# Self-attention: TensorE's transposes of the exponentials go ahead of the output projection in each step

## The chip, the cores and the metric

The kernel runs on one core of one Trainium2 chip. The metric is the device time in microseconds (us) from launch to the last store. Five engines work side by side and meet through semaphores: PE (TensorE: matmuls and transposes; PEld is its weight load, which overlaps them), DVE (VectorE), ACT (ScalarE), POOL (GpSimd) and SP (SyncE, which issues DMAs).

## What is computed

Four transformer blocks in a row over 64 sequences of 64 tokens with 256 features. The change lies in the causal self-attention of blocks 1 and 3, which is the same code called twice:

```python
x = rms_norm(hidden_states, ln_in_w)
mixed = jnp.where(vm, x @ v_qkv, x @ l_qkv)          # two experts, chosen by token
q, k, v = heads(q), heads(k), heads(v)               # 16 heads of 16
q, k = apply_rotary(q, k, position_ids, l)
ctx = sdpa(q, k, v, causal=True)                     # softmax(q k^T / 4) v
attn_out = jnp.where(vm, ctx @ v_dense, ctx @ l_dense)
hidden_states = residual + attn_out
```

## The kernel before

The 64 sequences are worked as 32 pairs of 64 + 64 tokens, so one pair fills 128 partitions. The nine phases of the network run one after the other (`layer0`, `self_attention(1)`, cross attention, gated feed-forward, latent attention, GELU feed-forward, `self_attention(3)`, cross attention, gated feed-forward). All engines wait for the last residual of a phase (`previous_done`) before they begin the next.

Inside `self_attention` every engine has its own hand-written list, and the order of the calls in it is the order on the engine. There is no scheduler. The lists are software pipelines: in step p of its loop (p = 0 to 33), PE has, before the change,

- `scores(p)` (L1021, L1029): two bf16 matmuls that write the causal mask into `ps_s`, and 16 matmuls on 64x64 tiles for q k^T;
- `dense(p - 2)` (L1075 to L1077): the output projection, six 128x512 matmuls into bank `ps_b`;
- `probs_t(p - 1)` (L1043): eight transposes of the exponentials into banks `ps_p` and `ps_d`;
- `proj_qk(p + 2)` (L984 to L986): twelve 128x512 matmuls into `ps_a`;
- `pv(p - 1)` (L1059): 64 small matmuls, exponentials times v;
- `xt_(p + 3)` (L972), `proj_v(p + 2)` (L1000 to L1002), `out_t(p - 1)` (L1066) and `qk_t(p + 2)` (L1013).

Calls whose pair lies outside 0 to 31 are left out. So steps 0 and 1 have no `dense`, steps 30 and 31 have no projections, step 32 has only `dense(30)`, `probs_t(31)`, `pv(31)` and `out_t(31)`, and step 33 only `dense(31)`.

The waits that matter here:

- `probs_t(p - 1)` waits for the exponentials (`exp_ok`, ACT L524) and for `on_ok` (DVE L1288). Its second four transposes also wait for `qkt_ok` up to pair p + 2, the copy of `ps_d` by ACT (L1154, `qkt_copy`) after `qk_t(p + 2)`, the last thing PE did in the step before.
- ACT copies the transposed exponentials out of both banks (L1162, `pt_copy`), and then makes the exponentials of pair p (L524). `pv(p - 1)` waits for both copies.
- `dense(p - 2)` waits for `o_ok`: `out_t` on PE, then `out_high` on ACT (L1169), then `out_low` on DVE (L1294). From pair 29 on it also waits for the residual before it.
- DVE takes `dense`'s result in `residual(p - 2)` (L1300, L1303), between `softmax_front(p)` (L510, L516) and `rope_products(p + 2)` (L1271). `proj_v(p + 2)` writes `ps_b` again and waits for that residual.

Of the kernel before, what the change touches and what calls it, by code (L numbers as in the profile page):

```python
# [107 lines left out]
def build(nc, t):  # L108
    with ExitStack() as ctx:
# [173 lines left out]
        def has(p):  # L283

            return not isinstance(p, int) or 0 <= p < PAIRS
# [626 lines left out]
        def self_attention(n, loaded, load_next):  # L912
            with ExitStack() as own:
# [50 lines left out]
                def _(pe):  # L964
                    previous_done(pe)
                    def xt_(p):
                        pe.wait_ge(xn_ok.handle, xn_ok.at(p + 1))
                        if xlow_ok.due(p):
                            pe.wait_ge(xlow_ok.handle, xlow_ok.at(p))
                        for c in range(CH):  # L970
                            for e in range(2):
                                ins = nc.tensor.transpose(ps_t[:, (2 * c + e) * P:(2 * c + e + 1) * P],  # L972
                                                          xn[:, e, c * P:c * P + P], ident)
                        ins.then_inc(xt_pe.handle, 1)

                    def proj_qk(p):

                        pe.wait_ge(xlow_ok.handle, xlow_ok.at(p + 1))
                        if rope1.due(p):
                            pe.wait_ge(rope1.handle, rope1.at(p))  # L980
                        u = p % 2
                        for k in range(2 * CH):
                            e, c = divmod(k, CH)
                            nc.tensor.matmul(ps_a[:], xh[:, u, c, e], wh[:, k, 0:2 * D], start=(k == 0), stop=False)  # L984
                            nc.tensor.matmul(ps_a[:], xh[:, u, c, e], wl[:, k, 0:2 * D], start=False, stop=False)  # L985
                            ins = nc.tensor.matmul(ps_a[:], xl[:, u, c, e], wh[:, k, 0:2 * D], start=False,  # L986
                                                   stop=(k == 2 * CH - 1))
                        ins.then_inc(qk_pe.handle, 1)

                    def proj_v(p):  # L990

                        if v_ok.due(p):
                            pe.wait_ge(v_ok.handle, v_ok.at(p))
                        if res_ok.due(p - 3):
                            pe.wait_ge(res_ok.handle, res_ok.at(p - 3))
                        u = p % 2
                        for k in range(2 * CH):
                            e, c = divmod(k, CH)
                            out = ps_b[:, 0:D]
                            nc.tensor.matmul(out, xh[:, u, c, e], wh[:, k, 2 * D:3 * D], start=(k == 0), stop=False)  # L1000
                            nc.tensor.matmul(out, xh[:, u, c, e], wl[:, k, 2 * D:3 * D], start=False, stop=False)
                            ins = nc.tensor.matmul(out, xl[:, u, c, e], wh[:, k, 2 * D:3 * D], start=False,  # L1002
                                                   stop=(k == 2 * CH - 1))
                        ins.then_inc(v_pe.handle, 1)
# [11 lines left out]
                    def scores(p):  # L1016
                        pe.wait_ge(kx_ok.handle, kx_ok.at(p + 1))
                        if sub_ok.due(p):
                            pe.wait_ge(sub_ok.handle, sub_ok.at(p))
                        for r in range(2):  # L1020
                            nc.tensor.matmul(ps_s[:, 512 * r:512 * r + 512], ident_b[:],  # L1021
                                             causal_b[:].unsqueeze(1).broadcast_to([P, 8, S]),
                                             start=True, stop=False, skip_group_check=True)
                        for r in range(2):
                            rows = slice(S * r, S * r + S)
                            for c in range(CH):
                                for b in range(2):
                                    at = 512 * r + 256 * c
                                    ins = nc.tensor.matmul(ps_s[b * S:b * S + S, at:at + 4 * S],  # L1029
                                                           qkt[rows, p % 2, c, b * S:b * S + S],  # L1030
                                                           kx[rows, p % 2, c, b].rearrange("p h k -> p (h k)"),
                                                           start=False, stop=True, skip_group_check=True)
                            ins.then_inc(s_pe.handle, 1)

                    def probs_t(p):
                        for r, bank in enumerate((ps_p, ps_d)):
                            pe.wait_ge(exp_ok.handle, exp_ok.at(p, r + 1))
                            if r == 0 and on_ok.due(p):
                                pe.wait_ge(on_ok.handle, on_ok.at(p))
                            if r == 1:  # L1040
                                pe.wait_ge(qkt_ok.handle, qkt_ok.at(min(p + 3, PAIRS)))
                            for j in range(4):
                                ins = nc.tensor.transpose(bank[:, j * P:j * P + P],  # L1043
                                                          probs[:, p % 2, (4 * r + j) * P:(4 * r + j + 1) * P], ident)
                            ins.then_inc(pt_pe.handle, 1)

                    def pv(p):

                        pe.wait_ge(pt_ok.handle, pt_ok.at(p + 1))
                        wait_slot(pe, p)  # L1050
                        if o_ok.due(p):
                            pe.wait_ge(o_ok.handle, o_ok.at(p))
                        for j in range(J):
                            at = 4 * (j % 4 // 2) + 2 * (j // 4) + j % 2
                            for h in range(2):
                                rows = slice(S * h, S * h + S)
                                for b in range(2):
                                    v = (v_own if b == h else v_swap)[rows, p % VS, 2 * j + h]
                                    ins = nc.tensor.matmul(o_at[b * S:b * S + S, h, j], pt[rows, at, b * S:b * S + S], v,  # L1059
                                                           start=True, stop=True, skip_group_check=True)  # L1060
                        ins.then_inc(pv_pe.handle, 2)
# [7 lines left out]
                    def dense(p):  # L1069
                        pe.wait_ge(o_ok.handle, o_ok.at(p + 1))  # L1070
                        pe.wait_ge(v_ok.handle, v_ok.at(min(p + 4, PAIRS)))
                        if p >= PAIRS - 3:
                            pe.wait_ge(res_ok.handle, res_ok.at(p))
                        for c in range(CH):
                            nc.tensor.matmul(ps_b[:], oth[:, c], oh[:, c], start=(c == 0), stop=False)  # L1075
                            nc.tensor.matmul(ps_b[:], oth[:, c], ol[:, c], start=False, stop=False)
                            ins = nc.tensor.matmul(ps_b[:], otl[:, c], oh[:, c], start=False, stop=(c == CH - 1))  # L1077
                        ins.then_inc(d_pe.handle, 1)
# [12 lines left out]
                    for p in range(PAIRS + 2):  # L1091
                        if has(p):
                            scores(p)
                        if has(p - 2):
                            dense(p - 2)
                        if has(p - 1):
                            probs_t(p - 1)
                        if has(p + 2):
                            proj_qk(p + 2)
                        if has(p - 1):  # L1100
                            pv(p - 1)
                        if has(p + 3):
                            xt_(p + 3)
                        if has(p + 2):
                            proj_v(p + 2)
                        if has(p - 1):
                            out_t(p - 1)
                        if has(p + 2):
                            qk_t(p + 2)
# [1550 lines left out]
```

## Time and profile before

| | us |
|---|---|
| Time, median of 3 runs (lowest, highest) | 2440.89 (2437.07, 2441.07) |
| Time of the profiled execution | 2433.26 |
| Its span, first to last instruction | 2431.5 |
| PE busy | 2269.9 (93%) |
| DVE busy | 1401.2 (58%) |
| ACT busy | 1142.3 (47%) |
| POOL busy | 653.4 (27%) |

The profile shows one execution. Busy time says how long an engine had work in hand. It does not say that the engine's work set the end: for that one reads the stage in question in order of time, and asks at each start whether the instruction waited for another engine or only for its turn. The mean TensorE clock granted over the span was 0.966 of full speed. The first self-attention phase lies at about 171 to 523 us of the span, the second at about 1651 to 2004 us.

### The profile page before, as it was taken

How to read it: one execution, taken by the hardware profiler on the slowest of the kernel's cores; microseconds unless marked ns; L12 is line 12 of the kernel's file. 1: busy time of each engine (PE TensorE's matmuls, PEld its weight loads, DVE VectorE, ACT ScalarE, POOL GpSimd, SP SyncE). 2: the span in 40 equal slices, each digit the busy share in tenths (PEclk: the TensorE clock that was granted, in tenths of full speed). 3: DMA queues.
4: the chain of work that ended last, by engine and by line, in shares of the span. 5: the costliest groups of instructions: out<-in, count | busy, mean ns of one | idle time of the engine just before them, and what ended most of it. 6: DMA issues, size and time to landing. Idle time of an engine off the chain costs nothing.

```text
span 2431.5 us, 62427 instructions
## 1 busy us (share of the span) xinstructions
PE 2269.9 (93%) x24066; PEld 1841.4 (76%) x24067; DVE 1401.2 (58%) x2837; ACT 1142.3 (47%) x2617; POOL 653.4 (27%) x833
## 2 busy tenths in 40 slices
PE   5969999979979997999999979998999989998998
PEld 3647888857659996788888859996888866667998
DVE  4756666647763333666666555545666655764333
ACT  3765445437653332444344335445455436664333
POOL 1552222226642221111111110002222215652222
PEclk9989999979989998999999989998999998999999
DMA  6620000020022113000000010000000002001111
GB/s 199 81 37 18 16 16 15 14 76 24 28 82 61 58 58 129 5 2 2 2 2 2 2 36 1 0 0 19 16 16 13 16 13 83 26 30 59 58 58 42
DMA packets 78750, 85.79 MB, mean 35 GB/s; under 512 B 19907, under 2 KB 69648, under 8 KB 78384
## 3 DMA queue, kind: packets, MB, share of 16 engines
q1 hardware_dynamic: 56016, 41.55, 7.3%
q10 hardware_dynamic: 14128, 19.74, 2.6%
q0 software_dynamic: 8368, 21.15, 2.4%
q8 instruction: 172, 2.82, 0.5%
q14 instruction: 66, 0.54, 0.1%
HBM read 52.35 MB, written 21.40 MB: 30 GB/s over the span
## 4 chain that ended last, share of the span: by engine, by line
PE 85%; DVE 4%; ACT 2%; issue 1%; ACTq 1%; POOL 0%; DMA 0%; POOLq 0%; DVEq 0%; SPq 0%
PE ps_all L2200 3%; PE ps_all L2202 3%; PE ps_all L2201 3%; PE ps_all L1431 3%; PE ps_all L1059 3%; PE ps_all L1457 3%; PE ps_all L1029 3%; PE ps_all L1832 3%; PE ps_all L1443 3%; PE ps_all L984 3%; PE ps_all L985 2%; PE ps_all L986 2%; PE ps_all L1043 2%; PE ps_all L2225 2%; PE ps_all L2227 2%; PE ps_all L2226 2%
## 5 line engine op out<-in xcount | busy, mean ns | idle before, releaser
L1224 POOL TENSOR_TENSOR s_kx<-s_qkt,const 128x512 f32<-128x512 f32 x128 | 131.6, 1049 | 448.0 <-ACT s_qkt L1154 448.0
L539 POOL TENSOR_TENSOR a_probs<-a_probs,a_sm 128x1024 f32<-128x1024 f32 x32 | 60.9, 1904 | 385.0 <-DVE a_sm L534 385.0
L1580 POOL TENSOR_TENSOR c_kx<-c_qkt,const 128x512 f32<-128x512 f32 x128 | 130.6, 1037 | 118.1 <-ACT c_qkt L1523 117.9
L2200 PE MATMUL ps_all<-f_wh,f_xh 128*128 x396 | 154.4, 390 | 5.3 <-DVE f_xl L2348 5.3
L1162 ACT ACTIVATE s_pt<-ps_all 128x512 f32<-128x512 f32 x128 | 69.6, 595 | 185.8 <-PE ps_all L1043 185.8
L2201 PE MATMUL ps_all<-f_wh,f_xl 128*128 x396 | 148.5, 375 | 0.0
L2202 PE MATMUL ps_all<-f_wl,f_xh 128*128 x396 | 148.5, 375 | 0.0
L1921 ACT ACTIVATE self_w<-ps_all,a_q_bias 128x256 f32<-128x256 f32 x128 | 53.8, 471 | 196.7 <-PE ps_all L1768 196.7
L2343 DVE SCALAR_TENSOR_TENSOR f_h<-ps_all,rstd,f_act_g 128x688 f32<-128x688 f32 x66 | 61.7, 935 | 142.0 <-PE ps_all L2202 128.9
L2225 PE MATMUL ps_all<-f_dh,f_hh 128*128 x396 | 116.9, 295 | 4.0 <-DVE f_hl L2358 4.0
L510 DVE TENSOR_REDUCE s_mx<-ps_all 128x8 f32<-128x512 f32 x128 | 82.5, 686 | 60.6 <-PE ps_all L1029 60.6
L2264 ACT ACTIVATE f_act_g<-ps_all,rstd 128x688 f32<-128x688 f32 x66 | 55.2, 837 | 131.8 <-PE ps_all L2202 131.7
L2269 ACT ACTIVATE f_hh<-ps_all 128x768 fp32r<-128x768 f32 x66 | 53.7, 813 | 132.4 <-PE ps_all L2210 132.4
L1271 DVE TENSOR_TENSOR s_roped<-ps_all,rope 128x512 f32<-128x512 f32 x64 | 44.3, 692 | 120.2 <-PE ps_all L986 120.2
L984 PE MATMUL ps_all<-s_wh,s_xh 128*128 128x512 f32 x256 | 107.2, 419 | 6.5 <-DVE s_xl L1256 6.5
L2227 PE MATMUL ps_all<-f_dl,f_hh 128*128 x396 | 111.6, 282 | 0.0
L2226 PE MATMUL ps_all<-f_dh,f_hl 128*128 x396 | 111.3, 281 | 0.0
L1531 ACT ACTIVATE c_pt<-ps_all 128x512 f32<-128x512 f32 x128 | 69.5, 594 | 82.6 <-PE ps_all L1443 82.6
L1630 DVE TENSOR_REDUCE c_mx<-ps_all 128x8 f32<-128x512 f32 x128 | 82.5, 686 | 44.7 <-PE ps_all L1431 44.5
L1136 ACT ACTIVATE s_xh<-ps_all 128x512 fp32r<-128x512 f32 x64 | 38.4, 600 | 143.8 <-PE ps_all L972 143.8
L985 PE MATMUL ps_all<-s_wl,s_xh 128*128 128x512 f32 x256 | 101.6, 397 | 0.0
L986 PE MATMUL ps_all<-s_wh,s_xl 128*128 128x512 f32 x256 | 101.5, 396 | 0.0
(319 smaller groups left out, 7423.6 us busy)
## 6 DMA issues: line engine op xcount, KB each, us to landing
s_v_swap<-s_v_own SPq DMA_DIRECT2D x128, 68.0 KB, 2.1
f_x_in<-x_sorted SPq DMA_DIRECT2D x66, 128.0 KB, 2.0
x_res<-x_sorted SPq DMA_DIRECT2D x66, 128.0 KB, 2.1
x_sorted<-x_res POOLq DMA_DIRECT2D x1, 4224.0 KB, 17.2
l_rows<-in_x SPq DMA_DIRECT2D x32, 128.0 KB
x_res<-in_x SPq DMA_DIRECT2D x32, 128.0 KB
x_res<-x_back SPq DMA_DIRECT2D x1, 3584.0 KB, 14.4
l_rows<-in_ctx SPq DMA_DIRECT2D x32, 64.0 KB
```

The costliest lines, as they stand in the source:

```text
L510: nc.vector.tensor_reduce(mx[:, u, half(r)], s3[:, half(r)], op=ALU.max, axis=AX.X) \
L984: nc.tensor.matmul(ps_a[:], xh[:, u, c, e], wh[:, k, 0:2 * D], start=(k == 0), stop=False)
L985: nc.tensor.matmul(ps_a[:], xh[:, u, c, e], wl[:, k, 0:2 * D], start=False, stop=False)
L986: ins = nc.tensor.matmul(ps_a[:], xl[:, u, c, e], wh[:, k, 0:2 * D], start=False, stop=(k == 2 * CH - 1))
L1224: ins = nc.gpsimd.tensor_tensor(kx[:, p % 2, c], qkt[:, p % 2, 2 + c].rearrange("p (b k) -> p b k", b=2).unsqueeze(2) .broadcast_to([P, 2, ...
L1580: ins = nc.gpsimd.tensor_tensor(kx[:, p % 2, b], qkt[:, p % 2, 1, b * S:b * S + S].unsqueeze(1).broadcast_to([P, RH, S]), const[:, C_H8X:C ...
L2200: nc.tensor.matmul(bank, x_high, wh[:, w_at], start=(c == 0), stop=False)
L2201: nc.tensor.matmul(bank, x_low, wh[:, w_at], start=False, stop=False)
L2202: ins = nc.tensor.matmul(bank, x_high, wl[:, w_at], start=False, stop=(c == CH - 1))
L2225: nc.tensor.matmul(bank, high, dh[:, w_at], start=(m == 0), stop=False)
L2226: nc.tensor.matmul(bank, low, dh[:, w_at], start=False, stop=False)
L2227: ins = nc.tensor.matmul(bank, high, dl[:, w_at], start=False, stop=(m == IC - 1))
```

## The change

In PE's list `probs_t(p - 1)` and `dense(p - 2)` change places. Nothing else does: the other engines' lists, the semaphores and the number of instructions are the same.

```diff
                     for p in range(PAIRS + 2):
                         if has(p):
                             scores(p)
+                        if has(p - 1):
+                            probs_t(p - 1)
                         if has(p - 2):
                             dense(p - 2)
-                        if has(p - 1):
-                            probs_t(p - 1)
                         if has(p + 2):
                             proj_qk(p + 2)
```

PE's rows in step 2 of the first self-attention, the first step that has both calls (- before, + after; the projection of pair 4, L984, follows):

```order
 L1021 MATMUL ps_all<-causal_b,ident_b 128x512
 L1029 MATMUL ps_all<-s_kx,s_qkt 64x256 x8
+L1043 MATMUL ps_all<-const,s_probs 128x128 [waits on_ok,exp_ok]
+L1043 MATMUL ps_all<-const,s_probs 128x128 x3
+L1043 MATMUL ps_all<-const,s_probs 128x128 [waits qkt_ok,exp_ok]
+L1043 MATMUL ps_all<-const,s_probs 128x128 x3
 L1075 MATMUL ps_all<-s_oh,s_oth 128x512 [waits v_ok,o_ok]
 L1076 MATMUL ps_all<-s_ol,s_oth 128x512
```

The eight transposes (L1043) stand between the scores and the six matmuls of the projection (L1075 to L1077), and the projection of q and k comes directly behind those. Steps 3 to 31 are alike in this.

PE's rows in step 32 of the first self-attention, where no scores and no projection of q and k are left:

```order
 L1066 MATMUL ps_all<-const,s_on 128x128 [waits on_ok]
 L1066 MATMUL ps_all<-const,s_on 128x128
+L1043 MATMUL ps_all<-const,s_probs 128x128 [waits on_ok,exp_ok]
+L1043 MATMUL ps_all<-const,s_probs 128x128 x3
+L1043 MATMUL ps_all<-const,s_probs 128x128 [waits qkt_ok,exp_ok]
+L1043 MATMUL ps_all<-const,s_probs 128x128 x3
 L1075 MATMUL ps_all<-s_oh,s_oth 128x512 [waits res_ok,v_ok,o_ok]
 L1076 MATMUL ps_all<-s_ol,s_oth 128x512
```

The transposes of pair 31 now stand directly behind `out_t(30)` (L1066) and ahead of `dense(30)`, whose first matmul waits for `o_ok`, which hangs on that same `out_t(30)`.

## Rows read from the trace of the kernel before

**Rows 1.** The page, part 4: shares of the span in the chain that ended last

```profile
PE 85%; DVE 4%; ACT 2%; issue 1%; ACTq 1%; POOL 0%; DMA 0%; POOLq 0%; DVEq 0%; SPq 0%
```

**Rows 2.** Windows, middle of self-attention: length; PE, PEld, DVE, ACT, POOL busy; PEclk; DMA

```profile
240.00:400.00 160.00, 160.00 (x2031) 128.93 (x2029) 106.14 (x216) 80.02 (x186) 36.49 (x42) 1.00 0.06 15
```

**Rows 3.** Timeline, PE, one middle step and the next one's start: start, length, what

```profile
309.03 0.59 PE L1021 MATMUL ps_all<-causal_b,ident_b 128*128 128x512 bf16 x2
...
310.59 0.50 PE L1075 MATMUL ps_all<-s_oh,s_oth 128*128 128x512 f32 x1
310.93 0.39 PE L1076 MATMUL ps_all<-s_ol,s_oth 128*128 128x512 f32 x1
...
312.09 1.03 PE L1043 MATMUL ps_all<-const,s_probs 128*128 128x128 f32 x8
312.88 0.48 PE L984 MATMUL ps_all<-s_wh,s_xh 128*128 128x512 f32 x1
...
313.43 0.39 PE L986 MATMUL ps_all<-s_wh,s_xl 128*128 128x512 f32 x1
...
315.48 0.39 PE L986 MATMUL ps_all<-s_wh,s_xl 128*128 128x512 f32 x1
315.80 0.23 PE L1059 MATMUL ps_all<-s_v_own,s_pt 64*64 64x17 f32 x1
...
319.42 0.59 PE L1021 MATMUL ps_all<-causal_b,ident_b 128*128 128x512 bf16 x2
```

**Rows 4.** Timeline, PE, step 1, which has no output projection

```profile
196.15 0.59 PE L1021 MATMUL ps_all<-causal_b,ident_b 128*128 128x512 bf16 x2
...
197.71 1.09 PE L1043 MATMUL ps_all<-const,s_probs 128*128 128x128 f32 x8
198.56 0.48 PE L984 MATMUL ps_all<-s_wh,s_xh 128*128 128x512 f32 x1
...
199.11 0.39 PE L986 MATMUL ps_all<-s_wh,s_xl 128*128 128x512 f32 x1
```

**Rows 5.** Waits, whole span: waiting group <- releaser: us in total, times, longest

```profile
PEld ps_all L1075 <- issue: 22.4, 58, 0.4
```

**Rows 6.** Timeline, ACT and DVE in the step of rows 3

```profile
309.23 0.60 ACT L1154 ACTIVATE s_qkt<-ps_all 128x512 f32<-128x512 f32 x1
313.70 1.15 ACT L524 ACTIVATE s_probs<-s_probs 128x512 f32<-128x512 f32 x2
...
313.08 0.47 DVE L1300 SCALAR_TENSOR_TENSOR s_part<-ps_all,vm,x_res 128x256 f32<-128x256 f32 x1
...
315.90 0.69 DVE L1271 TENSOR_TENSOR s_roped<-ps_all,rope 128x512 f32<-128x512 f32 x1 [1.82 <-PE ps_all L986]
```

**Rows 7.** Timeline, PE, steps 30 and 32 of the first self-attention

```profile
495.72 0.59 PE L1021 MATMUL ps_all<-causal_b,ident_b 128*128 128x512 bf16 x2
...
498.79 1.03 PE L1043 MATMUL ps_all<-const,s_probs 128*128 128x128 f32 x8
500.56 0.23 PE L1059 MATMUL ps_all<-s_v_own,s_pt 64*64 64x17 f32 x1 [0.74 <-ACT s_pt L1162]
...
509.60 0.44 PE L1066 MATMUL ps_all<-const,s_on 128*128 128x128 f32 x2 [0.84 <-DVE s_on L1288]
...
511.04 0.79 PE L1075 MATMUL ps_all<-s_oh,s_oth 128*128 128x512 f32 x1 [1.00 <-DVE s_otl L1294]
...
513.76 1.23 PE L1043 MATMUL ps_all<-const,s_probs 128*128 128x128 f32 x8
515.73 0.23 PE L1059 MATMUL ps_all<-s_v_own,s_pt 64*64 64x17 f32 x1 [0.74 <-ACT s_pt L1162]
```

**Rows 8.** Windows at the end of the first self-attention, columns as in rows 2

```profile
507.30:510.70 3.40, 1.56 (x66) 1.23 (x66) 1.34 (x5) 1.70 (x4) 0.00 (x0) 1.00 0.02 5
510.70:514.10 3.40, 3.06 (x8) 2.38 (x9) 0.38 (x2) 0.00 (x0) 0.00 (x0) 0.51 0.00 0
514.10:517.50 3.40, 2.01 (x72) 1.68 (x70) 1.41 (x4) 1.09 (x2) 0.00 (x0) 0.99 0.00 0
```

## The prediction

> **What bounds the kernel now.** I first read the shares of the chain that ended last: PE holds 85% of the span, DVE 4%, ACT 2% [rows 1]. Then I ask which engine sets the pace in the stage that the change touches. In 160 us from the middle of the first self-attention PE is busy 160.00 of 160.00 us at full granted clock, while DVE has 106.14, ACT 80.02 and POOL 36.49 [rows 2]. So in a middle step no other engine is waited for, and a reordering can only gain there what TensorE itself loses between one kind of work and the next. Third, I read one middle step in order of time. It takes 319.42 - 309.03 = 10.39 us [rows 3]. Fourth, I look at steps 30 to 33, where the projections have run out: there PE does wait, 0.74 us for ACT's copies before `pv` (L1059), 0.84 us for DVE before `out_t` (L1066), 1.00 us for DVE before `dense` [rows 7]. The reader is to see two different regimes: 28 steps in each phase (2 to 29) paced by PE's own work, and a few last steps paced by a chain through PE, ACT and DVE.
>
> **Part 1: the middle steps.** Nothing is added or removed, so only the seams between groups count. Before, the start of the third matmul of `proj_qk` lies at 313.43 - 309.03 = 4.40 us in the step [rows 3]. Now the same point after the change:
> - Transposes directly behind the scores: step 1 shows this, since it has no `dense`. They start at 197.71 - 196.15 = 1.56 us, and the next group follows 198.56 - 197.71 = 0.85 us later [rows 4], against 312.88 - 312.09 = 0.79 in a middle step [rows 3].
> - So `dense` starts at 1.56 + 0.85 = 2.41. The same kind of matmul directly behind transposes needs 0.55 us from its first to its third start (312.88 to 313.43, and 198.56 to 199.11) [rows 3, 4].
> - All further 128x512 matmuls, those of `dense` and then of `proj_qk`, follow in a steady rhythm: (315.48 - 313.43) / 9 = 0.228 us [rows 3]. From the third of `dense` to the third of `proj_qk` there are six intervals, 1.37 us.
>
> The sum is 2.41 + 0.55 + 1.37 = 4.33, so 0.07 us less than 4.40. The reason can be read from the rows: the first `dense` matmul behind the scores takes 310.93 - 310.59 = 0.34 instead of 0.23 us, and PEld stood idle 0.4 us before it, 58 times [rows 3, 5]. A large matmul there pays for its weight load in the open. A transpose pays only 0.06 (0.85 against 0.79), and the large matmuls then form one unbroken run of 18. 56 steps (28 in each phase) times 0.07 = 4 us. Bounds: nothing, if the seam costs the same whatever follows the scores. At the other end 0.11 us, the whole surcharge, makes 6 us. I take 4, since both orders of neighbours stand in the rows.
>
> The Trainium skill ("TensorE: Matmul & The Clock Gate", section "Step-by-step: what each phase is for") says that TensorE pulls a weight load ahead of matmuls in flight, so the next weights load while the current tile computes. By that rule the order of the groups would not matter and this term would be 0. The row of the weight load's idle time before L1075 differs from it at this seam, so the sum keeps 4.
>
> What covers the waits: the second four transposes wait for ACT's copy of `ps_d`, which ends at 309.23 + 0.60 - 309.03 = 0.80 us in the step [rows 6]. They would now start at about 1.56 + 0.85/2 = 1.99 us, so 1.2 us of cover are left of the 2.7 before. The exponentials were ready much earlier (L524 of the step before ended about 10.39 - (314.85 - 309.03) = 4.6 us ahead of the step's start) [rows 6]. `dense` ends later: its last matmul starts at 2.41 + 0.55 + 3 x 0.228 = 3.64 us. DVE's residual starts at 313.08 - 309.03 = 4.05 now, and would start near 4.1. Behind it DVE has 1.82 us of idle time before L1271, which waits for PE [rows 6]. That delay costs nothing. If the cover on DVE were gone, `proj_qk` of the next step would be late by the same 0.1 us. ACT's copies and the exponentials move about 1.5 us earlier, which nobody on the bounding engine waits for in these steps.
>
> **Part 2: steps 30 and 31.** Without `proj_qk`, `pv` follows the transposes by ACT's two copies: 500.56 - 498.79 = 1.77 us [rows 7]. Before, `dense` (1.50 us, 310.59 to 312.09 [rows 3]) stood in front of that chain, and `pv` started at 500.56 - 495.72 = 4.84 us in the step. After, `dense` lies beside the copies. The chain by the copies: 1.56 + 0.06 + 1.77 = 3.39. The chain by PE: `dense` starts at 2.41, and from the first large matmul behind transposes to `pv` it is (315.80 - 312.88) - 6 x 0.228 = 1.55 us for six of them [rows 3], so 3.96. The later one decides: 4.84 - 3.96 = 0.88 us less. Four such steps give 3.5 us. DVE must fit the residual in before `out_norm`. By the starts above, that fits with about 0.1 us to spare. If not, this term loses 0.4 us in all.
>
> **Part 3: step 32.** Before: `out_t(30)` at 509.60, then 1.44 us until `dense(30)` (through ACT and DVE), 2.72 us until the transposes, 1.97 until `pv(31)` at 515.73, in all 6.13 us [rows 7]. After, the eight transposes and ACT's copies run inside the 1.44 us and beside `dense`: the copies' chain is about 0.25 + 0.06 + 1.77 = 2.1 us. The path is then 1.44 + `dense` + nothing. With `dense` at full clock it is 1.44 + 1.57 = 3.01, a gain of 3.1. At half clock, as in the rows (PEclk 0.51 from 510.7 to 514.1 [rows 8]), it is 1.44 + 2.72 + 0.2 = 4.36, a gain of 1.8. I can't tell which of the two levels (2.4 or 1.2 GHz) holds there, so I take the middle, 2.4, and 4.8 us for both phases. Steps 0, 1 and 33 are unchanged. The second self-attention has the same list, so the same terms. The next phase waits for the last residual, so what is gained reaches the end.
>
> **The sum.** 4 + 3.5 + 4.8 = 12.3 us. The profiled execution took 2433.26 us (span 2431.5), so it would take 2421.0. It lies 7.6 us below the median of the three runs, 2440.89. Against the median the forecast is 2440.89 - 12.3 = 2428.6 us, rounded 2428.5. (0.2%, or 4.9 us, is about what a measurement of this kernel can tell from no change.)
>
> **The rivals.**
> - **The seam is worth nothing** (chance 0.20). The 58 weight-load gaps of 0.4 us [rows 5] may simply move with the scores, and the first transpose then pays what the first `dense` paid. Only parts 2 and 3 remain, 8.3 us: 2432.6. Against it: rows 4. The page on TensorE named above speaks for this one.
> - **The clock takes it back** (0.12). The granted clock went to half after a stretch in which PE was busy 1.56 of 3.40 us [rows 8]. The transposes moved into the gaps of steps 30 to 32 might not count for it, and steps 31 to 33 could see two more such stretches at half in each phase. One stretch of 3.4 us full of PE work costs 1.7 us, four cost 6.8: 12.3 - 6.8 = 5.5, so 2435.4, and a little more of it ends within 0.2%. The Trainium skill (same page, "Part 4: PE-mode transpose") says that transposes don't count as PE being busy. No row here separates them from other work.
> - **The transposes meet a wait of their own: slower** (0.04). The second four wait for ACT's copy of `ps_d`. That copy would have to end at 2.0 us in the step instead of 0.80, for example because another long ACT operation slipped ahead of it. Every microsecond beyond the cover is a microsecond of PE in each of 56 steps. It decides from 1.2 + 0.07 + (3.5 + 4.8 + 4.9)/56 (0.24, what parts 2 and 3 give and the bound of 0.2%) = 1.5 us of delay. At 1.6 us the steps lose 0.33 each, 18 us, less the 8.3 from the ends: 2451. Against it: ACT does this copy right when PE delivers, its list is unchanged, and it is busy half the time [rows 2].
> - **My forecast**: 0.64.
>
> **How the numbers follow.** Faster by over 0.2%: my forecast and the rival without the seam, nearly whole (0.60 + 0.19), and half of the clock's (0.06), 0.85. Within 0.2%: 0.11. Slower: 0.04. The range: the low end is the profiled execution's own level less the largest sum from the bounds (6 + 3.5 + 6.2 = 15.7, 2433.3 - 15.7 = 2418). The high end takes in the clock rival, 2435.4, and a little of the spread of the runs shown (2437.07 to 2441.07): 2437.
>
> **What the profile after would show.** A middle step of 10.32 us instead of 10.39, transposes at 1.56 us, `dense` at 2.41, and six intervals of 0.23 between the third matmul of `dense` and the third of `proj_qk`. PEld's 0.4 us of idle time stands before L1043. ACT's L1162 comes some 1.5 us earlier, DVE's L1300 at about 4.1. In steps 30 and 31 the wait of L1059 for ACT is gone, in step 32 `pv` comes 3.0 to 4.4 us behind `out_t`. Wrong would be: a wait of L1043 for ACT L1154, a middle step that is not shorter, or half-clock stretches that begin before step 32.

## The result and the profile after

| | before | after |
|---|---|---|
| Time, median of 4 runs (lowest, highest), us | 2440.98 (2437.07, 2448.52) | 2422.36 (2419.70, 2426.89) |
| Ratio after / before, 95% interval | | 0.9922 (0.9893 to 0.9951) |
| Profiled execution, us | 2433.26 | 2426.89 |
| Span, mean granted clock | 2431.5, 0.966 | 2425.1, 0.970 |

The kernel got faster by 18.6 us between the medians, 0.78%. The forecast was 12.3 us, or 2428.5 as a median, the range 2418 to 2437. Two later sets of the changed kernel gave 0.9924 (0.9908 to 0.9941) and 0.9934 (0.9921 to 0.9948).

The first lines of the page of after have the form of the table ahead of the prediction and of [rows 1]:

```profile
PE 2264.3 (93%) x24066; PEld 1839.5 (76%) x24067; DVE 1402.9 (58%) x2837; ACT 1153.0 (48%) x2617; POOL 655.0 (27%) x833
...
PE 85%; DVE 4%; ACT 2%; issue 1%; ACTq 1%; POOL 0%; DMA 0%; POOLq 0%; DVEq 0%; SPq 0%
```

These shares hardly moved and tell nothing of where 6.4 us of span went, so the stage itself has to be read. Timeline of after, PE, the same middle step as in [rows 3], to the start of the next:

```profile
308.17 0.59 PE L1021 MATMUL ps_all<-causal_b,ident_b 128*128 128x512 bf16 x2
...
309.73 1.09 PE L1043 MATMUL ps_all<-const,s_probs 128*128 128x128 f32 x8
310.58 0.48 PE L1075 MATMUL ps_all<-s_oh,s_oth 128*128 128x512 f32 x1
310.89 0.39 PE L1076 MATMUL ps_all<-s_ol,s_oth 128*128 128x512 f32 x1
...
312.52 0.40 PE L986 MATMUL ps_all<-s_wh,s_xl 128*128 128x512 f32 x1
...
313.67 0.39 PE L985 MATMUL ps_all<-s_wl,s_xh 128*128 128x512 f32 x1
...
314.58 0.39 PE L986 MATMUL ps_all<-s_wh,s_xl 128*128 128x512 f32 x1
314.89 0.23 PE L1059 MATMUL ps_all<-s_v_own,s_pt 64*64 64x17 f32 x1
...
318.52 0.59 PE L1021 MATMUL ps_all<-causal_b,ident_b 128*128 128x512 bf16 x2
```

The step takes 10.35 us instead of 10.39. The transposes start at 1.56, `dense` at 2.41, the third matmul of `proj_qk` at 4.35, as worked out to within 0.02 us (1.56, 2.41, 4.33). But from the second matmul of `dense` to the eighth of `proj_qk` (310.89 to 313.67) the twelve intervals average 0.232 us, and only the last four (313.67 to 314.58) are 0.228.

Before the change `dense` already had this slower rhythm. Its last matmul in the step of [rows 3] (timeline of before, PE):

```profile
311.86 0.40 PE L1077 MATMUL ps_all<-s_oh,s_otl 128*128 128x512 f32 x1
```

From its second matmul (310.93 [rows 3]) to this sixth one there are four intervals in 0.93 us, 0.233 us each, where `proj_qk` had 0.228.

The wait of the weight load moved with the seam, as its row in the list of waits shows ([rows 5] had L1075, 22.4 us, 58 times):

```profile
PEld ps_all L1043 <- issue: 23.9, 62, 0.4
```

ACT and DVE in that step, timeline of after, against [rows 6]:

```profile
308.37 0.60 ACT L1154 ACTIVATE s_qkt<-ps_all 128x512 f32<-128x512 f32 x1
310.42 1.08 ACT L1162 ACTIVATE s_pt<-ps_all 128x512 f32<-128x512 f32 x2 [1.46 <-PE ps_all L1043]
...
312.25 0.48 DVE L1300 SCALAR_TENSOR_TENSOR s_part<-ps_all,vm,x_res 128x256 f32<-128x256 f32 x1
...
315.00 0.69 DVE L1271 TENSOR_TENSOR s_roped<-ps_all,rope 128x512 f32<-128x512 f32 x1 [1.74 <-PE ps_all L986]
```

ACT's copy L1154 ends 0.80 us into the step, before the transposes start at 1.56, so nothing waits. ACT's L1162 starts at 2.25, 1.45 us earlier than before. DVE's residual starts at 4.08 (forecast 4.1, before 4.05), and DVE still idles 1.74 us behind it.

The last steps of the first self-attention, timeline of after, PE ([rows 7] are those of before):

```profile
504.50 0.59 PE L1021 MATMUL ps_all<-causal_b,ident_b 128*128 128x512 bf16 x2
...
506.06 1.09 PE L1043 MATMUL ps_all<-const,s_probs 128*128 128x128 f32 x8
506.90 0.48 PE L1075 MATMUL ps_all<-s_oh,s_oth 128*128 128x512 f32 x1
...
508.47 0.23 PE L1059 MATMUL ps_all<-s_v_own,s_pt 64*64 64x17 f32 x1
...
516.64 0.44 PE L1066 MATMUL ps_all<-const,s_on 128*128 128x128 f32 x2 [0.84 <-DVE s_on L1288]
516.92 1.04 PE L1043 MATMUL ps_all<-const,s_probs 128*128 128x128 f32 x8
518.09 0.50 PE L1075 MATMUL ps_all<-s_oh,s_oth 128*128 128x512 f32 x1
...
519.68 0.23 PE L1059 MATMUL ps_all<-s_v_own,s_pt 64*64 64x17 f32 x1
...
521.64 0.44 PE L1066 MATMUL ps_all<-const,s_on 128*128 128x128 f32 x2 [0.84 <-DVE s_on L1288]
523.08 0.50 PE L1075 MATMUL ps_all<-s_oh,s_oth 128*128 128x512 f32 x1 [1.00 <-DVE s_otl L1294]
```

Step 30: `pv` starts 3.97 us into the step instead of 4.84, and its wait for ACT is gone. Step 32: from `out_t(30)` at 516.64 to `pv(31)` it is 3.04 us instead of 6.13. The waits for DVE ahead of L1066 and the last L1075 stay, since nothing was put into them. Windows of after, columns as in [rows 2]:

```profile
517.40:520.80 3.40, 3.27 (x76) 2.39 (x73) 1.39 (x3) 1.19 (x3) 0.00 (x0) 1.00 0.02 5
520.80:524.20 3.40, 1.56 (x8) 1.14 (x8) 1.11 (x3) 0.38 (x1) 0.00 (x0) 1.00 0.00 0
528.20:541.80 13.60, 7.58 (x32) 5.03 (x32) 1.92 (x4) 3.72 (x13) 5.26 (x6) 0.50 1.05 304
...
1995.90:2016.40 20.50, 12.33 (x54) 6.78 (x53) 4.82 (x12) 6.11 (x19) 7.41 (x9) 0.50 0.62 206
```

Both `dense(30)` (from 518.09) and `dense(31)` (from 523.08) of this phase ran at the full level, where before the clock was at half from 510.7 to 514.1 us [rows 8] and again from 517.6 us. It falls only at 528.2, when the phase is over (it ends at 525.8). In the second self-attention, which ends at 1997.5 us, it fell at 1995.9, in the last matmul of `dense(31)`.

Cut at PE's own starts, the two self-attention phases of both profiles come apart like this (worked out from the traces, us):

```
                                             before           after
first L972 to scores(2)                   33.91  34.44     34.45  34.23
scores(2) to scores(30), 28 steps        290.63 290.63    289.51 289.51
scores(30) to out_t(30)                   13.87  13.88     12.15  12.15
out_t(30) to pv(31)                        6.13   6.25      3.03   3.03
pv(31) to dense(31)                        3.65   3.40      3.40   3.40
dense(31) to the next phase                4.02   4.03      2.76   2.95
phase                                    352.22 352.63    345.30 345.26
```

### The profile page after: what moved, and what is told of

Its sections match the earlier page's. It is cut to its first block, busy times and chain, and to the rows that moved or that the text cites. A ratio compares the mean times of both kernels' runs of the same rounds, so it can differ in the third digit from the quotient of the medians.

```text
span 2425.1 us, 62427 instructions
## 1 busy us (share of the span) xinstructions
PE 2264.3 (93%) x24066; PEld 1839.5 (76%) x24067; DVE 1402.9 (58%) x2837; ACT 1153.0 (48%) x2617; POOL 655.0 (27%) x833
## 4 chain that ended last, share of the span: by engine, by line
PE 85%; DVE 4%; ACT 2%; issue 1%; ACTq 1%; POOL 0%; DMA 0%; POOLq 0%; DVEq 0%; SPq 0%
PE ps_all L2202 3%; PE ps_all L2201 3%; PE ps_all L2200 3%; PE ps_all L1059 3%; PE ps_all L1457 3%; PE ps_all L1431 3%; PE ps_all L1029 3%; PE ps_all L1043 3%; PE ps_all L1832 3%; PE ps_all L1443 3%; PE ps_all L984 3%; PE ps_all L985 2%; PE ps_all L986 2%; PE ps_all L2225 2%; PE ps_all L2227 2%; PE ps_all L2226 2%
## 5 line engine op out<-in xcount | busy, mean ns | idle before, releaser
L1162 ACT ACTIVATE s_pt<-ps_all 128x512 f32<-128x512 f32 x128 | 69.5, 596 | 90.9 <-PE ps_all L1043 90.8
L984 PE MATMUL ps_all<-s_wh,s_xh 128*128 128x512 f32 x256 | 102.7, 401 | 6.5 <-DVE s_xl L1256 6.5
```

## The experiments

The lengths of stretches, which the experiments are read by, are worked out from the traces. A phase of self-attention runs from its first PE instruction (L972) to the first PE instruction of the next phase. The stretch ahead of it (column "ahead") runs from the first L633 on PE, the start of `layer0`, to the first self-attention.

```
kernel           ratio to before (95%)       ahead   phase 1   phase 3 (us)
before                                       144.5   352.22    352.63
before_again     0.9997 (0.9987 to 1.0006)   152.2   352.38    352.74
mid_only         0.9992 (0.9982 to 1.0001)   146.6   350.84    353.35
steps3031_only   0.9966 (0.9952 to 0.9980)   146.1   349.45    349.49
step32_only      0.9959 (0.9944 to 0.9973)   148.5   347.71    348.20
tail_only        0.9949 (0.9932 to 0.9965)   151.9   346.80    347.04
after            0.9922 (0.9893 to 0.9951)   153.3   345.30    345.26
after_again      0.9924 (0.9908 to 0.9941)   148.0   345.24    345.33
after_third      0.9934 (0.9921 to 0.9948)   148.6   345.23    345.35
early_scores31   0.9940 (0.9922 to 0.9957)   146.2   347.14    345.13
qk_first         0.9932 (0.9918 to 0.9945)   146.3   345.51    345.48
front_sbuf       (one run, 2419.93 us)       147.2   345.22    345.32
```

("Phase 3" is the second self-attention, that of block 3.)

**before_again**, the kernel before without an edit.

> The kernel before, unchanged, once more. All theories: ratio 1 within its interval. What it is for: how far the time up to the first self-attention (171 us in the profile of before, 181 in that of after, with nothing changed there) moves by itself. If that is chance, this run's first self-attention starts somewhere between 165 and 185 us, its length is 352 to 353 us as before, and steps 30 to 32 look as before.

Measured: ratio 0.9997. The first self-attention starts at 178.6 us, where the first profile had 171.2. Where each began and where the last `dense` was, for this kernel and below for the changed one (first and last start of a line's instructions; L1077 within the first 700 us):

```profile
L972 PE MATMUL ps_all<-const,s_xn x256: 270/273/448, 178.6 to 1972.1; 128*128 128x128 f32 x128
...
L1077 PE MATMUL ps_all<-s_oh,s_otl x64: 393/398/628, 214.8 to 529.3; 128*128 128x512 f32 x64
```

```profile
L972 PE MATMUL ps_all<-const,s_xn x256: 270/273/448, 180.5 to 1963.8; 128*128 128x128 f32 x128
...
L1077 PE MATMUL ps_all<-s_oh,s_otl x64: 390/395/399, 217.9 to 524.3; 128*128 128x512 f32 x64
```

From the first to the last L1077 it is 314.5 us before and 306.4 after. The stretch ahead of self-attention varies by 9 us from one execution to another, in kernels that don't differ there (144.5 to 153.3 in the table), while a phase repeats to 0.2 us as long as the clock does. Part of the 9 us is DMA: L633 waits for `x_res` 14.7 us in all in the first profile of before and 19.8 us in that of after. So the 6.4 us between the two spans understate the change: after's profile had the longest such stretch of all, before's the shortest. The two phases together are (352.22 + 352.63) - (345.30 + 345.26) = 14.3 us shorter.

**tail_only**, the new order in steps 30 to 32 alone. In it and the three that follow, a condition on p chooses the order:

```diff
+                        if has(p - 1) and (p >= 30):
+                            probs_t(p - 1)
                         if has(p - 2):
                             dense(p - 2)
-                        if has(p - 1):
+                        if has(p - 1) and not (p >= 30):
                             probs_t(p - 1)
```

> The new order only in steps 30 to 32, the old one in steps 2 to 29. If the gain comes mostly from the last steps (my theory, with the profile after: 0.86 us for each of steps 30 and 31, 3.1 us for step 32, 1.5 us for dense(31) at full clock), each self-attention phase gets 6.3 us shorter and the kernel 12.6 us, ratio 0.995. If the gain were one of the middle steps, this run is within 0.1% of before. Half clock at the end of the phases should be gone as in the profile after.

Measured: ratio 0.9949 (12.4 us), phases 5.4 and 5.6 us shorter, 11 of the 14.3. In the first phase the clock fell just ahead of `dense(31)`, against the expectation. Windows of this kernel:

```profile
517.60:521.00 3.40, 2.18 (x69) 1.43 (x68) 1.65 (x4) 0.35 (x1) 0.00 (x0) 1.00 0.02 5
521.00:524.40 3.40, 2.78 (x6) 1.82 (x6) 0.42 (x1) 0.04 (x1) 0.00 (x0) 0.50 0.00 0
```

`dense(31)`, whose first matmul starts at 521.62, then runs at half: from its start to the next phase it is 4.02 us instead of the 2.76 in after. In the second phase the clock fell within `dense(31)`, and it is 3.35. This is mostly why the phases miss the expected 6.3 us by 0.9 and 0.7.

**mid_only**, `p < 30` in the condition.

> The new order only in steps 2 to 29, the old one in steps 30 to 32. If the middle steps give 0.04 us each (what the profile after shows), the phases get 1.1 us shorter each, 2.2 us in all, ratio 0.999. If they gave what the whole change measured beyond the last steps (18.6 less 12.6), it would be 6 us, ratio 0.9975. Steps 30 to 32 as before, with their waits.

Measured: ratio 0.9992 (1.9 us, but the interval includes no change at all). The profile is sharper than the times: the middle step is 10.353 us instead of 10.393 in steps 2 to 28 of both phases, and step 29, which has no `xt_`, 9.967 instead of 10.007. The first phase is 1.4 us shorter. The second came out 0.6 to 0.7 longer, since one more stretch at half fell into its step 31, as these windows of the kernel show:

```profile
1984.00:1987.90 3.90, 3.90 (x24) 1.84 (x24) 1.16 (x3) 0.38 (x1) 0.00 (x0) 0.62 0.02 4
1987.90:1991.30 3.40, 2.66 (x76) 2.24 (x74) 2.63 (x5) 2.10 (x4) 0.00 (x0) 1.00 0.00 0
```

So the middle steps are worth 0.040 us each, 2.2 us in all, and not the 6 us of the other theory.

**steps3031_only**, `p in (30, 31)`.

> The new order only in steps 30 and 31 of both phases. By part 2 of the prediction, 0.88 us for each of the four, 3.5 us in all, phase length 350.6 us. Together with step 32 alone (phase lengths 347.7 and 348.2) and the middle alone (350.8 and 353.4) this shows whether the parts add up to 345.3. The half-clock stretches of step 32 and of the end stay as before.

Measured: 0.9966, phases 349.45 and 349.49, 2.8 and 3.1 us shorter where 1.8 was expected. From `scores(30)` to `out_t(30)` it is 12.15 us, as in after. The rest came from the clock, which had not been expected to move. Windows of this kernel:

```profile
510.00:513.00 3.00, 2.00 (x12) 1.56 (x11) 0.59 (x2) 0.38 (x1) 0.00 (x0) 1.00 0.03 5
...
516.30:523.00 6.70, 4.31 (x10) 2.42 (x10) 2.08 (x8) 0.38 (x1) 0.10 (x1) 0.50 0.00 0
```

`dense(30)`, in its old place in this kernel (511.13), ran at full clock in both phases. That the steps before it had become denser is the likely reason, since nothing else differs from before.

**step32_only**, `p == 32`.

> The new order only in step 32 of both self-attention phases. If the wait chain behind out_t(30) takes pv(31) with it and the granted clock stays full, 3.1 us come from step 32 and 1.5 us from dense(31) at full clock: 4.6 us a phase, 9.2 us in all, ratio 0.996, phase length 347.7 us. If the clock does not follow (half level as before), 1.8 us a phase, 3.6 us in all, phase length 350.5 us.

Measured: 0.9959, phases 347.71 and 348.20. The first of the two expectations, to 0.5 us. Timeline of this kernel, PE:

```profile
513.35 0.44 PE L1066 MATMUL ps_all<-const,s_on 128*128 128x128 f32 x2 [0.84 <-DVE s_on L1290]
513.63 1.04 PE L1043 MATMUL ps_all<-const,s_probs 128*128 128x128 f32 x8
514.79 0.50 PE L1075 MATMUL ps_all<-s_oh,s_oth 128*128 128x512 f32 x1
...
516.38 0.23 PE L1059 MATMUL ps_all<-s_v_own,s_pt 64*64 64x17 f32 x1
...
519.78 0.50 PE L1075 MATMUL ps_all<-s_oh,s_oth 128*128 128x512 f32 x1 [1.00 <-DVE s_otl L1296]
```

The same 3.03 us from `out_t(30)` to `pv(31)`, and `dense(31)` at full clock. One window of this kernel:

```profile
511.20:514.60 3.40, 2.37 (x74) 2.10 (x74) 1.36 (x4) 1.89 (x5) 0.00 (x0) 1.00 0.03 5
```

Up to `out_t(30)` this kernel ran as before. There the clock fell 1.14 us behind the start of `out_t(30)` (510.74), after 3.40 us in which PE had been busy for 1.56 [rows 8]. Here PE was busy for 2.37 of the 3.40 us up to the same place. What was added are the transposes (from 513.63), and the clock did not fall. This was so in both phases, while in all six phases measured with the old steps 30 to 32 the clock fell 1.1 to 2.4 us behind `out_t(30)`. That speaks for transposes counting as work for the clock. It is no proof, since the moment of the fall moves from one execution to the next. One moved call in one step (times two phases) brings some 9 us, 60% of the whole. The parts overlap: steps 30 and 31 alone (2.9 a phase) and step 32 alone (4.5) would add up to 7.4, together they give 5.5. Each alone already brings `dense(30)` to full clock, which is worth 1.4 us and can be won only once, and in tail_only `dense(31)` was at half again, wholly in one phase and in part in the other.

**after_again** and **after_third**, the changed kernel.

> The changed kernel once more, beside the other three. If the parts add up: 14.5 us faster than before, ratio 0.994 (12.6 from the last steps, 2.2 from the middle ones). If the 18.6 us between the two medians were all the change's, ratio 0.9922 again and a phase length below 345 us.

> The changed kernel a third time, as the partner of early_scores31 and to narrow the ratio. By the lengths of the phases in the profiles, 14.4 us faster than before, ratio 0.994. By the two medians so far, 16 to 19 us, 0.992 to 0.993. Phase length 345.3 us both times.

Measured: 0.9924 and 0.9934, phases 345.2 to 345.4 in both. By the phases the change is worth 14.4 us, 0.59% (ratio 0.9941). That lies inside the intervals of the first and third set and at the very edge of the second. Three medians say 16 to 19 us; the 18.6 of the first set rests on four runs of before with a median of 2440.98, where the later sets of 11 to 19 runs had 2436.6 to 2438.0. What lies behind the start of the first self-attention, without the two phases, took 1555.4 us in both profiles of before and 1554.0, 1555.4 and 1555.3 in the three of after, so no further gain stands there. The rest of the difference would have to lie ahead of self-attention, where executions differ by 9 us, or be chance. Which of the two is not shown.

**early_scores31**, the changed kernel with the scores of pair 31 ahead of `out_t(29)`.

```diff
+                        if p == PAIRS - 2:
+                            scores(p + 1)
                         if has(p - 1):
                             out_t(p - 1)
```

(and `scores(p)` at the head of the step is left out for p = 31).

> The changed kernel, and in step 30 the scores of pair 31 go ahead of out_t(29), into the 0.84 us in which PE waits for DVE there. If that wait is a real hole in the path, step 31 starts about 0.8 us earlier in each phase: 1.6 us, ratio to before 0.9935 where the changed kernel has 0.994. If DVE (front of pair 31 behind out_norm(29)) sets the pace instead, nothing.

Measured: 0.9940 (0.9922 to 0.9957), no better than after. `pv(30)` follows `pv(29)` by 5.66 us instead of 6.22, so the hole was filled. But `out_t(30)` follows `pv(30)` by 2.33 us instead of 1.96, so 0.18 is left of it. `out_t(29)` now stands behind the scores (502.67), DVE's `out_low(29)` waits for it, and the front of pair 31 is queued behind that on DVE, although its scores were ready. Timeline of this kernel, DVE:

```profile
503.63 0.42 DVE L1296 TENSOR_TENSOR s_otl<-ps_all,s_oth 128x256 fp32r<-128x256 f32 x1 [1.68 <-ACT s_oth L1171]
503.97 1.28 DVE L510 TENSOR_REDUCE s_mx<-ps_all 128x8 f32<-128x512 f32 x2
```

The second phase gained some 0.2 us, and the first lost 1.9 to a stretch at half clock. Windows of this kernel, and its timeline, PE:

```profile
507.30:510.70 3.40, 2.67 (x13) 2.37 (x14) 1.06 (x4) 1.58 (x3) 0.00 (x0) 0.72 0.02 5
508.80:512.20 3.40, 3.40 (x11) 2.37 (x9) 0.42 (x1) 1.28 (x3) 0.00 (x0) 0.50 0.02 5
```

```profile
508.03 0.44 PE L1066 MATMUL ps_all<-const,s_on 128*128 128x128 f32 x2 [1.21 <-DVE s_on L1290]
...
512.29 0.23 PE L1059 MATMUL ps_all<-s_v_own,s_pt 64*64 64x17 f32 x1
```

Here `dense(30)` ran at half in the new order, and from `out_t(30)` to `pv(31)` it is 4.26 us instead of 3.03.

**front_sbuf**, the changed kernel with DVE reading other numbers from SBUF in self-attention.

```diff
-                            softmax_front(dve, mx, probs, p, p % 2)
+                            softmax_front(dve, mx, probs, p, p % 2, self_w[:, 0:NH * S])
```

> The changed kernel with one thing altered in self-attention: DVE's maxima and subtractions (L510, L516) read 1024 columns of the raw weights in SBUF in place of the scores in PSUM, so its attention is that of other numbers. It asks why twelve of the large matmuls in a middle step follow at 0.230 to 0.236 us instead of 0.227, which is why the middle step gained 0.04 and not 0.07 us. If DVE's reads of PSUM slow TensorE's writes, the intervals of dense and of the first six of proj_qk fall to 0.227 and a middle step takes 10.31 us. If not, they stay, and the step stays at 10.35.

Measured: the middle step stays at 10.353 us, interval by interval. Timeline of this kernel, PE:

```profile
303.95 0.39 PE L1076 MATMUL ps_all<-s_ol,s_oth 128*128 128x512 f32 x1
...
306.73 0.39 PE L985 MATMUL ps_all<-s_wl,s_xh 128*128 128x512 f32 x1
...
307.64 0.39 PE L986 MATMUL ps_all<-s_wh,s_xl 128*128 128x512 f32 x1
```

Again 2.78 us for twelve intervals and 0.91 for four. DVE's reads of the scores in PSUM are not the reason. The other reads of PSUM, ACT's and those of DVE's residual, were left as they were here.

**qk_first**, the changed kernel with `proj_qk` ahead of `dense`, and on DVE `rope_products` ahead of `residual`.

```diff
-                        if has(p - 2):
-                            dense(p - 2)
                         if has(p + 2):
                             proj_qk(p + 2)
+                        if has(p - 2):
+                            dense(p - 2)
```

> The changed kernel with proj_qk ahead of dense (PE: scores, transposes, proj_qk, dense), and DVE's rope_products ahead of its residual to fit. It asks what the intervals of 0.229 to 0.236 us hang on. If on the place (the first twelve after the transposes are slow whatever they are), the middle step stays at 10.355 us. If on the kind (proj_qk directly behind transposes has two slow intervals in step 1, dense has five everywhere), five fewer are slow and the middle step takes 10.33 us, 1.4 us in all over 56 steps. If residual and proj_v, which waits for it, become the bound, it is slower: half a microsecond a step would be 28 us, ratio above 1.

Measured: 0.9932, the middle step 10.353 us. Timeline of this kernel, PE:

```profile
302.62 0.48 PE L984 MATMUL ps_all<-s_wh,s_xh 128*128 128x512 f32 x1
...
303.40 0.39 PE L984 MATMUL ps_all<-s_wh,s_xh 128*128 128x512 f32 x1
...
305.44 0.40 PE L1075 MATMUL ps_all<-s_oh,s_oth 128*128 128x512 f32 x1
...
306.61 0.39 PE L1077 MATMUL ps_all<-s_oh,s_otl 128*128 128x512 f32 x1
```

Now `proj_qk`, directly behind the transposes, runs at 0.227 us an interval from its fourth on (303.40 to 305.44, nine intervals), and `dense` at 0.234 (305.44 to 306.61, five). So the slow intervals go with `dense` and what follows it, not with the place behind the transposes. The 18 large matmuls take 3.99 us from first to last start instead of 4.00. The 0.01 us is lost again between `proj_v` and `out_t`, so the step as a whole is the same and the expected 10.33 us did not come. Its phases are 0.2 us longer, in step 29 (10.13 us instead of 9.97). None of these versions beats the changed kernel.

## Why the prediction was right

**The two regimes** held: middle steps paced by PE alone, last steps by a chain through PE, ACT and DVE, and the larger part of the gain from the last ones. The mechanism is the one that was forecast. That the sum of 12.3 us lies near the 14.3 of the phases is in part luck, since two errors of opposite sign stand in it. The median, 2422.4 against 2428.5, lies 6 us off: 2 of them are in the phases, the other 4 are the part of the medians' difference that the phases don't hold.

**Part 1, the middle steps (forecast 4 us, measured 2.2).** The seams behave as worked out, to 0.02 us at every point up to the third matmul of `proj_qk`. The step that failed is "All further 128x512 matmuls, those of `dense` and then of `proj_qk`, follow in a steady rhythm", with 0.228 us for it. That rhythm was taken from nine late intervals of `proj_qk`. `dense` has its own of 0.233, which the trace of before already showed (310.93 to 311.86), and behind `dense` the first matmuls of `proj_qk` run at 0.229 to 0.235 too, where behind transposes only two did. That costs 0.03 us a step, about half of it up to the third matmul of `proj_qk` and half behind it. The rival "the seam is worth nothing" is refuted by 0.040 us in each of 56 steps, which mid_only shows by itself. The Trainium skill ("TensorE: Matmul & The Clock Gate", section "Step-by-step: what each phase is for") has the next weights loaded while the current tile computes. The trace differs from that at this seam: the weight load sat idle for 0.4 us, and the second matmul started after 0.34 us instead of 0.23. Why `dense` and its successor are slower stays open. The place behind the transposes is excluded by qk_first, DVE's reads of the scores in PSUM by front_sbuf. A different supply of weights or instructions was not tried.

**Part 2, steps 30 and 31 (forecast 0.88 each, measured 0.86).** `dense` lies beside ACT's copies, PE's own work decides, and DVE's residual fits.

**Part 3, step 32 (forecast 2.4 a phase, measured 3.1).** Both ends were computed right: 3.01 at full clock, 3.03 measured, and 4.36 at half, where the first phase of early_scores31 had 4.26. The 1.57 us for `dense` in the first sum stands in no row; it measured 1.59 (518.09 to 519.68). The forecast took the middle because the level could not be told, and it was the full one in both phases of all three profiles of the changed kernel.

**What was missed** is in the same part: "Steps 0, 1 and 33 are unchanged". Their instructions are, but `dense(31)` in step 33 ran at full instead of half clock, wholly in three of the six phases of the changed kernel and in part in the others. From its start to the next phase it was 4.02 us before and is 2.76 and 2.95 after (2.76 to 3.38 in the other two profiles of after). With 0.1 between `pv(31)` and `dense(31)` that is some 1.3 us a phase. The rival "the clock takes it back" had the sign wrong: packing the last steps holds the clock up, and the transposes in the gap did not keep it from that (step32_only speaks against the premise that they don't count). Over the span the half level lasted 166 and 173 us in the two profiles of before, 142 to 146 in the three of after.

The sum of what was measured: 2.2 + 4 x 0.86 + 2 x 3.1 + 2 x 1.3 = 14.4 us, against 14.3 by the lengths of the phases (their first stretch, unchanged, varies by half a microsecond). The forecast of 12.3 was 1.8 too high in part 1 and 4 too low in the last steps.

**The wait of the transposes** for ACT L1154 (the slower rival) never appears. The copy ends 0.8 us before even the first four start.

## What to carry to other kernels

In a software pipeline look at the last steps by themselves: where most groups have run out, two independent groups in the wrong order put one's work in front of the other's latency, and it costs microseconds although the middle of the loop is full and hides it. Put the group on whose result another engine has work to do first, and the one that only needs to be done by then behind it. A stretch that ends sooner and denser can also keep TensorE's clock up, so a fix there may bring more than its instructions.

When two profiles are compared, measure the stage and not the span: here the spans differed by 6.4 us and the changed stages by 14.3, because a stretch ahead of them, the same in both kernels, varies by 9 us.

## What was not expected of the hardware

- 128x512 matmuls of one shape and type follow at 0.227 us in one place and at 0.229 to 0.236 in another, exactly repeated in every step, and it depends on which group came before.
- Where a large matmul stands directly behind 64x64 work its second follows at 0.34 us. A transpose there costs 0.06 more than elsewhere, a large matmul 0.11.
- By packing the last steps closer, the half level of the clock at the end of a phase (before: 3.4 us at `dense(30)`, then 24 us from ahead of `dense(31)` on) became one stretch that began within `dense(31)` or behind the phase. It lasted 10 to 21 us in the six phases of the changed kernel.
